# An embedding bag by one-hot matmuls: table parting moved wholly to VectorE, one-hots built a chunk at a time, three sets of pair banks

## The reference, cut to what matters

```python
B, F, V, L, E = 512, 32, 12500, 20, 64
flat = tables.reshape(F * V, E)                       # float32
emb = flat[ids + arange(F)[None, :, None] * V]        # B x F x L x E
mask = (arange(L) < lengths[..., None])
pooled = einsum('bfle,bfl->bfe', emb, mask)
out = nan_to_num(pooled.reshape(B, F * E))
```

## Time and profile before

| | us |
|---|---|
| median of 3 runs (1184.69 to 1189.72) | 1185.06 |
| the profiled execution, first to last instruction | 1287.7 |

### The profile page before, as it was taken

One profiled execution on the slowest core, in us unless ns is written; L12 is line 12 of the kernel. 1 busy time (PEld: TensorE's weight loads), 2 busy tenths in 40 slices (PEclk: granted clock), 3 DMA queues, 4 the chain that ended last, 5 costly groups with the idle time before them and its releaser, 6 DMA issues.

```text
span 1287.7 us, 31751 instructions
## 1 busy us (share of the span) xinstructions
PE 1118.5 (87%) x10873; PEld 969.4 (75%) x10873; DVE 992.5 (77%) x2692; ACT 827.6 (64%) x1233; POOL 547.5 (43%) x519
## 2 busy tenths in 40 slices
PE   3379999896988878989979888979789999999996
PEld 1168888785876767778868767868678888888886
DVE  9657788884886867869868867969678898787881
ACT  4257787673756656757747566757557777787780
POOL 4865665556555455555565544555540101000000
PEclk9989999897999988999989989989989999999998
DMA  5324234241433333242414333242413213123120
GB/s 184 116 68 115 60 83 144 74 136 45 135 107 95 117 86 97 81 132 82 143 46 136 106 95 118 82 130 69 134 25 100 58 55 104 47 62 100 35 73 5
DMA packets 63916, 118.38 MB, mean 92 GB/s; under 512 B 30120, under 2 KB 31742, under 8 KB 63840
## 3 DMA queue, kind: packets, MB, share of 16 engines
q1 hardware_dynamic: 46608, 102.19, 25.5%
q0 software_dynamic: 16032, 15.00, 5.9%
q10 hardware_dynamic: 1200, 0.50, 0.2%
HBM read 87.19 MB, written 4.62 MB: 71 GB/s over the span
## 4 chain that ended last, share of the span: by engine, by line
PE 73%; DVE 10%; another core or an unknown queue 7%; ACT 7%; issue 3%; DVEq 0%; POOL 0%; POOLq 0%
PE sums L525 48%; PE pairs L515 19%; PE rest L543 6%; DVE onehot_j L742 3%; ACT counts L470 3%; ACT table L482 2%; DVE gathered L800 1%; DVE onehot_p L740 1%; ACT rest L478 1%; DVE table L751 1%; ACT table L486 0%; DVE table L759 0%; DVEq L796 0%; DVE is_nan L768 0%
## 5 line engine op out<-in xcount | busy, mean ns | idle before, releaser
L525 PE MATMUL sums<-table,counts 128*128 128x192 bf16 x8624 | 909.0, 251 | 0.8 <-issue 0.8
L470 ACT ACTIVATE counts<-pairs 128x588 int16<-128x588 f32 (+1 forms) x968 | 617.0, 650 | 368.9 <-PE pairs L515 262.7
L525 PEld LDWEIGHTS sums<-table,counts 128*128 128x128 fp8e3 x8624 | 776.3, 98 | 55.0 <-issue 0.4
L427 POOL DMA_INDIRECT rows<-tables,row_now x413 | 453.3, 1098 | 376.7 <-issue 206.1
L742 DVE TENSOR_SCALAR onehot_j<-ramp,j_of,worth 128x296 bf16<-128x296 f16 x1848 | 536.3, 353 | 0.0
L515 PE MATMUL pairs<-onehot_j,onehot_p 128*128 128x294 bf16 x1892 | 410.4, 297 | 112.8 <-ACT counts L470 67.3
L740 DVE TENSOR_TENSOR onehot_p<-ramp,p_of 128x768 bf16<-128x768 f16 x308 | 169.9, 552 | 253.7 <-PE pairs L515 172.9
L515 PEld LDWEIGHTS pairs<-onehot_j,onehot_p 128*128 128x128 bf16 x1892 | 178.2, 98 | 187.3 <-issue 107.8
L543 PE MATMUL rest<-table,minus_eye 128*128 128x448 bf16 x352 | 102.5, 373 | 38.2 <-ACT table L482 17.1
L486 ACT ACTIVATE table<-rest 128x896 f32<-128x896 f32 x88 | 80.8, 918 | 35.3 <-remote 23.6
L437 POOL DMA_INDIRECT out_gathered<-gathered,place_now x40 | 42.4, 1061 | 132.3 <-DVE gathered L771 121.0
(11 more groups left out here) (68 smaller groups left out, 79.8 us busy)
## 6 DMA issues: line engine op xcount, KB each, us to landing
table<-tables SPq DMA_DIRECT2D x154, 448.0 KB
rows<-zeros SPq DMA_DIRECT2D x40, 640.0 KB
rows<-tables,row_now POOLq DMA_INDIRECT x413
out_counted<-pooled SPq DMA_DIRECT2D x132, 21.0 KB
rows<-lookup_ids SPq DMA_DIRECT2D x1, 903.0 KB, 8.5
rows<-lookup_lengths SPq DMA_DIRECT2D x1, 903.0 KB, 10.2
out_counted<-pooled SPq DMA_DIRECT2D x44, 1.0 KB
sorted_records<-records,rank POOLq DMA_INDIRECT x40
```

Source lines behind the costliest of these rows:

```text
L427: nc.gpsimd.indirect_dma_start(out=rows[:, k, l * E:(l + 1) * E], out_offset=None, in_=table_rows, in_offset=bass.IndirectOffsetOnAxis(ap= ...
L470: nc.scalar.activation(dst, src, ACT.Copy).then_inc(counts_saved, 1)
L525: last = nc.tensor.matmul(sums[h][:, k * PARTS * E:(k + 1) * PARTS * E], counts[h][:, j, :, k], parts[:, :, j, :, 1], start=(j == 0 and k ...
```

## The change

- `PARTED` replaces the two tables: VectorE parts all seven chunks of a feature, chunk 0 at stage 4, then 5, 7, 8, 10, 11, 12. The path through `rest`, its matmuls and its three ScalarE copies a chunk go.
- The j one-hots of a stage are one `tensor_tensor` (`steps`), two groups side by side, against a doubled ramp (`ramp_j`, made once); before it stood six `tensor_scalar`.
- The weight 256 is no longer in `onehot_j`: ScalarE multiplies the p one-hots of a stage by it in place (`weigh`), issued after the eviction of the second pair of the stage before. `count` waits for both once a stage instead of for each group.
- A third set of pair banks, in the room of `rest`.
- Adds move to stages (0, 6, 13) and (3, 9); the last of the 40 falls into feature 18, stage 6. Cleaning moves from stage 10 to 9.

```diff
-SETS = 2
+SETS = 3
-PARTED_AT = {0: 9, 2: 16, 4: 24, 5: 29}
-PARTED_BY_VECTOR = {6: 1, 9: 3, 12: 6}
-ADDS = (0, 4, 13), (3, 11)
+PARTED = {4: 0, 5: 1, 7: 2, 8: 3, 10: 4, 11: 5, 12: 6}
+ADDS = (0, 6, 13), (3, 9)
-READ_FIRST, READ_SECOND, CLEAN = 1, CHUNKS + 1, CHUNKS + 3
+READ_FIRST, READ_SECOND, CLEAN = 1, CHUNKS + 1, CHUNKS + 2
...
+            def weigh(f, h, c):
+                s = onehot_set(h, c)
+                act.wait_ge(places_ready, f * STAGES + (h * CHUNKS + c + 1))
+                nc.scalar.activation(onehot_p[:, s, 1:, :, :], onehot_p[:, s, 1:, :, :], ACT.Copy,
+                                     scale=weight[:]).then_inc(weighted, 1)
...
                         for q in range(PAIRS):
                             save_counts(f, h, c, q)
-                            u = slot(h, c, q)
-                            if u - 2 in begun_in:
-                                save_low(f, begun_in[u - 2])
-                            if u - 1 in begun_in:
-                                save_middle(f, begun_in[u - 1])
-                            if u in begun_in:
-                                copy_chunk(f, begun_in[u])
+                            stage = h * CHUNKS + c + 1
+                            if q == PAIRS - 2 and (f, stage) < (M - 1, STAGES):
+                                weigh(f + stage // STAGES, stage // CHUNKS % 2, stage % CHUNKS)
...
+                if q == 0:
+                    pe.wait_ge(onehots_ready, onehots_of(f, h, c) + 1)
+                    pe.wait_ge(weighted, f * STAGES + (h * CHUNKS + c + 1))
+                    pe.sem_inc(count_begun, 1)
+                for x in range(2):
+                    last = nc.tensor.matmul(pair(h, c, q)[:, x, 0:WIDE], onehot_p[:, s, 1 + q, :, x],
+                                            onehot_j[:, s, q, :, x], start=True, stop=True)
...
+            def places(f, h, c):
+                stage = f * STAGES + h * CHUNKS + c
+                if stage >= AHEAD:
+                    dve.wait_ge(counted, eviction_at(stage - AHEAD, PAIRS - 1) + 1)
+                nc.vector.tensor_tensor(onehot_p[:, onehot_set(h, c), 1:, :, :],
+                                        ramp_twice.unsqueeze(1).to_broadcast([P, PAIRS, P, 2]), of_chunk(p_of, f, h, c, P),
+                                        ALU.is_equal).then_inc(places_ready, 1)
+            def steps(f, h, c):
+                nc.vector.tensor_tensor(onehot_j[:, onehot_set(h, c)],
+                                        ramp_j[:].unsqueeze(1).to_broadcast([P, PAIRS, WIDE, 2]), of_chunk(j_of, f, h, c, WIDE),
+                                        ALU.is_equal).then_inc(onehots_ready, 1)
...
-                for i in range(PER_CHUNK):
-                    onehots(f, h, c, i)
-                    if stage in PARTED_BY_VECTOR and i == 1:
-                        cut_rest(f, PARTED_BY_VECTOR[stage])
-                    if stage in PARTED_BY_VECTOR and i == 4:
-                        cut_low(f, PARTED_BY_VECTOR[stage])
+                places(f, h, c)
+                if stage in PARTED:
+                    cut_rest(f, PARTED[stage])
+                steps(f, h, c)
+                if stage in PARTED:
+                    cut_low(f, PARTED[stage])
```

More of the change, by code:

```diff
@@ L206, in build_embedding_bag @@
         pairs = [psum(f"pairs{s}", [P, 2, 512], F32) for s in range(SETS)]
-        rest = psum("rest", [P, 2, 512], F32)
         sums = [psum(f"sums{h}", [P, 512], F32) for h in range(2)]
@@ L265, in eviction_at @@
             return eviction(stage // STAGES, stage // CHUNKS % 2, stage % CHUNKS, q)
-        def slot(h, c, q):
-            return (h * CHUNKS + c) * PAIRS + q
-        by_vector = sorted(PARTED_BY_VECTOR.values())
-        begun_in = {u: c for c, u in PARTED_AT.items()}
-        PARTED = len(PARTED_AT)
-        def parted(f, c):
-            return f * PARTED + sorted(PARTED_AT).index(c) + 1
-        def halves_of(c):
-            return [slice(c * CE + x * CE // 2, c * CE + (x + 1) * CE // 2) for x in range(2)]
-        def both_halves(part, c):
-            return table[:, part, c * CE:(c + 1) * CE].rearrange("p (x n) -> p x n", x=2)
         def upper_halves(part):
@@ L509, in count @@
                     pe.wait_ge(counts_saved, free)
-                for x in range(1 if q < 0 else 2):
-                    i = -1 if q < 0 else 2 * q + x
-                    pe.wait_ge(onehots_ready, group(f, h, c, i) + 1)
-                    s = onehot_set(h, c, i)
-                    k, side = buffer_p(i)
-                    last = nc.tensor.matmul(pair(h, c, q)[:, x, 0:WIDE], onehot_p[:, s, k, :, side],
-                                            onehot_j[:, s, i + 1, 0:WIDE], start=True, stop=True)
+                if q < 0:
+                    s = onehot_set(h, -1)
+                    pe.wait_ge(onehots_ready, onehots_of(f, h, -1) + 1)
+                    nc.tensor.matmul(pair(h, c, q)[:, 0, 0:WIDE], onehot_p[:, s, 0, :, 0], single_j[:, s, 0:WIDE],
+                                     start=True, stop=True).then_inc(counted, 1)
+                    return
+                s = onehot_set(h, c)
+                if q == 0:
[5 more added lines that the diff above has]
+                                            onehot_j[:, s, q, :, x], start=True, stop=True)
                 last.then_inc(counted, 1)
@@ L591, in _ @@
             rank_lengths()
-            begin_rest()
             phase(0, 0, with_products=False)
@@ L683, in columns_of_lookups @@
                 step(nc.vector.tensor_scalar(b, a, float(TRIO), place[:, 1:2], ALU.mult, ALU.add))
-                step(nc.vector.scalar_tensor_tensor(out=j_of[:, part], in0=look_len[:, part], scalar=place[:, 0:1], in1=b,
+                step(nc.vector.scalar_tensor_tensor(out=j_of[:, halves, 0:GROUPS],
+                                                    in0=look_len[:, part].rearrange("p (h g) -> p h g", g=GROUPS),
+                                                    scalar=place[:, 0:1], in1=b.rearrange("p (h g) -> p h g", g=GROUPS),
                                                     op0=ALU.is_gt, op1=ALU.mult))
-                last = j_of[:, part].rearrange("p (h g) -> p h g", g=GROUPS)[:, :, LAST]
+                last = j_of[:, halves, LAST]
                 step(nc.vector.tensor_scalar(last, last, back_a_slot[:], None, ALU.add))
```

108 lines of the change are left out of this document (32 added, 76 removed).

## The result

The changed kernel takes 1262.0 us (median of 4, 1259.9 to 1267.6), the kernel before beside it 1187.4 (median of 4): a ratio of 1.063, with a 95% interval of 1.059 to 1.067. Slower was forecast, by 1.5%; it is 6.3%. The profiled execution has a span of 1260.2 us, 2.0 less than its own run (1262.2).

What follows compares the result with a forecast made beforehand. TensorE was taken as the bound, gathers barely ahead. Engine savings gave 1121 us, but slower gathers put the last add at 996; plus 193.5, 10 around the span and about 3 for the clock: 1203 us, 1.5% slower, range 1145 to 1270.

Steps and rivals of the forecast that it cites:

- What bounds the kernel now: Kernel before: TensorE is the bound late in the kernel; GpSimd's gathers run about 7 us (0 to 20) ahead of VectorE's need.
- TensorE, VectorE, ScalarE: Engine steps: a feature falls from 49.0 to 45.1 us, with adds from 50.0 to 47.4; `weigh` on ScalarE costs nothing.
- the working for `steps`: VectorE's single j one-hot operation of 1764 elements, estimated from L740 and L751: 1.07 to 1.9 us, taken as 1.07.
- The head of a half: TensorE's wait there for the eviction of the last pair of the half before: about 0.5 us instead of 0.80.
- GpSimd, the part that decides: Gathers slowed by `tensor_tensor`: pace from 2.00 to 2.16 us, last add at 996, 1203 us in all; forecast case 0.43.
- the model of single holds: A `tensor_tensor` running at a gather's early SBUF read holds it until its end: mean loss from 0.11 to 0.39 us.
- D: Rival: gathers cannot get in between back-to-back `tensor_tensor`, so a cut stage holds 3.48 us; pace 2.5, 1284 us; chance 0.10.
- Passing on: Share of a gather's delay reaching GpSimd's pace: about half, 0.16 us a gather (bounds 0.10 and 0.29).
- A: Rival: gathers are not slowed by `steps` and the cuts; last add at 946, total 1150 us; chance 0.18.
- B: Rival: GpSimd is 5 to 10% faster outside the profile; 1175 to 1121 us; chance 0.14.
- C: Rival: a gather's delay passes on in full, pace 2.29 us, total 1235 us; inside the range, no chance of its own.
- E: Rival: `steps` runs at one element a cycle, 13 us more a feature, over 1290 us; chance 0.03 shared with a slow `weigh`.

Runs made afterwards that it cites:

- e13: The kernel before, unedited, run once more with a profile, on a chip where it shows no stops of TensorE: 1189.2 us, ratio 0.997.
- e16: The changed kernel with only the adds moved, two a feature from tile 3 on, scatters at their old place: 1077.8 us, ratio 0.904 to the kernel before.
- e11: The changed kernel with a one-element `tensor_scalar` behind each of the four `tensor_tensor` of a stage with a cut: 1238.6 us, ratio 0.967 to the kernel before.
- e12: The changed kernel with spread adds, plus a one-element `tensor_scalar` behind each `tensor_tensor` of a stage with a cut: 1125.3 us, ratio 0.880 to the kernel before.
- e7: The changed kernel with the j one-hots of a chunk as six `tensor_scalar` again, with one operation each: median 1275.2 us of four runs.
- e9: The changed kernel with the j one-hots as six two-operation `tensor_scalar` a chunk, as in the kernel before: 1297.2 us, ratio 1.012 to the kernel before.
- e4: The changed kernel with adds spread two a feature from tile 3 on and each tile's last scatter one gather earlier: 1127.5 us, ratio 0.881 to the kernel before.

## Why the prediction was right and wrong

**The account that closes.** Between its first gather and its last scatters no wait of GpSimd is put down to VectorE, in e13 or after, so its line gives the time. From e13 to after: first gather 85.05 to 99.77, +14.7; first to last gather 871.5 to 937.9, +66.4; last gather to last add 18.9 to 26.0, +7.1; last add to the end of the span 211.6 to 196.6, -15.0. Sum 73.2; the spans differ by 1260.2 - 1187.0 = 73.2. The other way, by features: the engines save 2.7 us in each of 20 features and 2.6 in the last, 57; what the features exceed their calm length grows from 54 to 185 us. 185 is 47 more than the 138 of VectorE's waits. Some 37 of the 47 lie in the eight stretches with adds at stages 9, 0 and 6, 3.4 to 5.8 us in each, and the two of them that wait for no rows, at full clock, have as much (4.6) as the others. So this is mainly the adds pushing back the one-hots. The clock has a smaller part: behind the wait of tile 24 TensorE starts at the lower of its two levels (0.50 granted from 716 to 722, 1.00 from 725; 0.92 in the mean between 140 and 1064).

**What bounds the kernel now: wrong.** The number was right. The last add of an ordinary run was put at 962 to 972 and the gathers at 955; e13 has 975.4 and 956.5. But I read this as "about 7 us ahead", two chains that do not touch yet. They had touched five times, 57 us in all. With `add_rows` waiting for a scatter behind two more tiles, an add that stands 17 to 27 us behind its tile's last gather, as these five do, is already bound. The trace read could not show these waits, as its stops gave GpSimd time.

**TensorE, VectorE, ScalarE: right in kind, the saving too large.** Calm features: 45.1 forecast, 46.3 measured, from 49.0. With adds 47.4 was forecast from 50.0. e13 has 49.0 there where no add waits, so the adds cost the kernel before nothing, and the 50.0, read from the profile with stops, was too long; the changed kernel has 51.8 and 46.0 to 47.1 in turn, 49.2 in the mean. With adds at its own stages it saves nothing; with them spread (e16) it takes 46.3. GpSimd hid this part of the error, as VectorE would have waited anyway. In the working for `steps`, the upper bound of 1.9 us does not follow from 1.0 ns for each element more than L740 has (that gives 1.56); 1.071 is far from both. The head of a half costs 0.84 instead of 0.5, twice; the rest lies in the stages (3.18 to 3.19 instead of 3.15). `weigh` at 0.925 is just past its bound. TensorE at the head of a half, after:

```profile
1140.12 0.29 PE L478 MATMUL pairs<-single_j,onehot_p 128*128 128x294 bf16 x1
1140.96 0.42 PE L487 MATMUL pairs<-onehot_j,onehot_p 128*128 128x294 bf16 x2 [0.55 <-ACT counts L446]
```

**GpSimd, the part that decides: right in kind, too small.** This is the step that failed: the last add was to stand at 996, and it stands at 1063.6. Against the forecast's own terms: the start, +15.5 (first gather 99.8, not 84.3: no step asked what the cuts and `steps` do to the 40 record scatters, 1.147 us each in e13 and 1.486 now); the run of the gathers 937.9 instead of 912, +26; last gather to last add, taken as 0 because only rows were thought to be waited for, +26 (the last long wait is that of tile 36 for a scatter, and three adds follow it); the tail 198.4 instead of 206.5, -8 (about 2 us lie around the span, not 10). 1203 + 59 = 1262.

The 1.39 for a gather met 1.399 by luck. It was meant for gathers beside a working VectorE; those that met an idle VectorE or an add (96) took 1.00, and without such gathers the mean is about 1.5. The 394 gathers up to 2.2 us have a mean of 1.194, only 0.11 over e13, where the model of single holds gave 0.29 more; the other 19 take 107.4 us together, and they make up the rest. What is missing in the model are these unbroken rows of `tensor_tensor`, which stood under D. Passing on: while VectorE works, a gather takes (937.9 - 42 - 138) / 329 = 2.30 us, if the waits hold 83 gathers at the 1.67 of the earlier trace rows; forecast 2.16, e13 by the same count 2.04. So 0.26 passed on of a hold of some 0.4 (1.5 against 1.10 by the same count in e13), neither half nor all.

**Rivals.** A is refuted by the 1.399, B by e13, whose gathers come at (871.5 - 42) / 412 = 2.01 us, where I had 2.00. C gave the right pace, 2.29, by too large a share of too small a hold; its 1235 lacks the start and the scatter. D is real but rare: 19 of 413 gathers and some 25 us (e11, beside the changed kernel on other chips), not 100. E is refuted by the 1.071. The page of the Trainium skill named above infers that `tensor_tensor` does not hold up the making of descriptors. The scatter of 7.08 us shows that a DMA which GpSimd issues is held up all the same; whether in reading SBUF, where the same section has the two contend, or in making descriptors, no run separates.

## What to carry to other kernels

When the profiled execution is 8% longer than the runs, its slack is not slack: before weighing a faster engine, take a profile at the level of the times, or allow for a second chain that already touches. Ask of each wait what else the waiting instruction needs, here a scatter that another engine issues two tiles later. And where a helper engine keeps up only in the mean, move its consumers later before making anything faster, and to places where they do not push back the engine's own work: two constants brought the changed kernel from 1262 us to 1078, where the change alone had cost 75.

## What the runs showed of the hardware

- An indirect DMA that GpSimd issues while VectorE runs `tensor_tensor` back to back is mostly held to 0.87 us behind the one under way (143 of 162, mean 1.29 us, against 1.00 undisturbed), and at times to the end of the whole row (19, up to 11.0 us). With a one-element `tensor_scalar` in between the longest took 3.54 (e11) and 3.96 (e12).
- `tensor_scalar` of 296 elements with one SBUF tile as input did not hold such DMAs: 1.02 us beside the one-operation form (e7), 1.03 beside the form with two (e9).
- Lengths can lock: in e7 a held gather put the next one onto the next `tensor_tensor` 56 times, and the mean rose from 1.20 (e9) to 1.44 us.
- The same kernel differs by 6 to 8% between chips: TensorE stops for 3 to 8 us, up to 172 us of waits without a releaser over all engines in one trace and none in another. The kernel before suffers most; e16 and e4, nearly the same kernel, stand at 1078 and 1127.
- ScalarE, SBUF to SBUF, 768 elements bf16: 0.925 us, no less than 896 from f32.
